# Second attention: value-sum matmuls of a unit in one block, exponentials in two buffers, x parked in DRAM

## What is computed

```python
c_q  = x @ Wq_down                                    # 512 -> 64
c_kv = x @ Wkv_down
q_c = (c_q @ Wq_up).reshape(b, s, 128, 4)
q_r = (x @ Wq_rope).reshape(b, s, 128, 64)
k_c = (c_kv @ Wk_up).reshape(b, s, 128, 4)
v_c = (c_kv @ Wv_up).reshape(b, s, 128, 4)
k_r = x @ Wk_rope                                     # shared by all heads
scores = (einsum('bqhd,bkhd->bhqk', q_c, k_c) + einsum('bqhd,bkd->bhqk', q_r, k_r)) / sqrt(68)
out = einsum('bhqk,bkhd->bqhd', softmax(scores), v_c).reshape(b, s, 512) @ Wo
x = x + ga * out
```

## Time and profile before

| | us |
|---|---|
| median of 3 runs | 2480.24 |
| range of the runs | 2477.19 to 2480.72 |
| span of the profiled execution | 2475.1 |
| TensorE busy (matmuls) | 2315.8 (94%) |
| VectorE busy | 1807.3 (73%) |
| ScalarE busy | 1336.2 (54%) |
| GpSimd busy | 580.5 (23%) |

### The profile page before, as it was taken

How to read it: one execution, slowest core, us unless ns; L and a number is a source line. 1 busy time by engine, 2 the same in 40 slices (tenths; PEclk the granted TensorE clock), 3 DMA queues, 4 the chain that set the end, 5 groups by cost and what they waited for, 6 DMA issues and landing times.

```text
span 2475.1 us, 41157 instructions
## 1 busy us (share of the span) xinstructions
PE 2315.8 (94%) x11084; PEld 1674.6 (68%) x11084; DVE 1807.3 (73%) x3372; ACT 1336.2 (54%) x2583; POOL 580.5 (23%) x428
## 2 busy tenths in 40 slices
PE   6898898998998788999999999999999999999988
PEld 4677777777776555666666666666666666666655
DVE  6788889888887465676676776776776766767856
ACT  2333333333333324776676766766766766766641
POOL 4355545455544041000000000000000000001432
PEclk9899999999999888999999999999999999999998
DMA  5101001001003204111111111111111111112330
GB/s 192 44 26 43 17 25 42 17 25 42 17 0 86 79 1 155 33 38 38 36 37 37 33 36 38 36 37 37 32 37 38 36 37 33 37 37 69 107 82 35
DMA packets 114848, 113.31 MB, mean 46 GB/s; under 512 B 28669, under 2 KB 71197, under 8 KB 114796
## 3 DMA queue, kind: packets, MB, share of 16 engines
q1 hardware_dynamic: 114796, 112.66, 15.4%
HBM read 93.20 MB, written 18.87 MB: 45 GB/s over the span
## 4 chain that ended last, share of the span: by engine, by line
PE 73%; DVE 15%; ACT 4%; issue 3%; DMA 1%; SPq 1%; POOL 1%; DVEq 0%; POOLq 0%; ACTq 0%
PE bank L1773 11%; PE bank L1786 10%; PE bank L1799 10%; PE bank L1787 9%; PE bank L1761 5%; PE bank L1759 5%; PE bank L1760 5%; PE bank L1485 4%; PE bank L1487 4%; PE bank L1486 4%; ACT probs L817 3%; DVE probs L1147 3%; DVE probs L1134 2%; DVE nmax L1138 2%; PE bank L1573 2%
## 5 line engine op out<-in xcount | busy, mean ns | idle before, releaser
L1334 DVE TENSOR_REDUCE mcol<-bank 128x1 fp32r<-128x512 f32 x1024 | 702.3, 690 | 393.3 <-PE bank L1773 386.5
L958 ACT ACTIVATE pT<-bank 128x512 f32<-128x512 f32 x1024 | 598.9, 599 | 368.4 <-PE bank L1787 340.8
L1773 PE MATMUL bank<-km,q 128*128 128x512 f32 x1024 | 434.8, 426 | 5.7 <-DVE mcol L1334 3.4
L1786 PE MATMUL bank<-q,k 128*128 128x512 f32 x1024 | 418.5, 409 | 6.6 <-DVE c_lo L1305 3.2
L1773 PEld LDWEIGHTS bank<-km,q 128*128 128x128 f32 x1024 | 316.8, 310 | 155.5 <-DVE mcol L1334 113.1
L1787 PE MATMUL bank<-q,k 128*128 128x512 f32 x1024 | 405.8, 396 | 0.0
L697 POOL TENSOR_TENSOR wr_lo<-wst,wr_hi 128x512 fp32r<-128x512 f32 x64 | 82.6, 1291 | 1267.1 <-DVE wr_hi L1293 1267.1
L1786 PEld LDWEIGHTS bank<-q,k 128*128 128x128 f32 x1024 | 195.7, 191 | 131.0 <-ACT pT L958 108.2
L1799 PE MATMUL bank<-pT,vp 128*32 128x512 f32 x2048 | 272.7, 605 | 0.7 <-ACT pT L958 0.7
L1787 PEld LDWEIGHTS bank<-q,k 128*128 128x128 f32 x1024 | 192.8, 188 | 37.8
L1761 PE MATMUL bank<-hT_hi,wr_lo 128*128 128x512 f32 x512 | 207.0, 404 | 0.0
(11 more groups left out here) (266 smaller groups left out, 4056.8 us busy)
## 6 DMA issues: line engine op xcount, KB each, us to landing
wst<-in_L_attn_Wq_rope SPq DMA_DIRECT2D x64, 256.0 KB, 3.0
wm<-in_L_wmod SPq DMA_DIRECT2D x12, 1024.0 KB, 8.6
st_q<-in_L_attn_wq SPq DMA_DIRECT2D x8, 1024.0 KB, 7.4
st_wo<-in_L_attn_wo SPq DMA_DIRECT2D x8, 1024.0 KB, 5.2
km<-kc_d SPq DMA_DIRECT2D x256, 32.0 KB
q<-qc_d SPq DMA_DIRECT2D x256, 32.0 KB
k<-kc_d SPq DMA_DIRECT2D x256, 32.0 KB
o_d<-ost SPq DMA_DIRECT2D x512, 16.0 KB
```

What stands on the lines that cost most here:

```text
L958: act.activation(pT[:, s], bank[s % 4][:], ACT.Exp, scale=float((HD1 + ROPE) ** -0.5)).then_inc(exp1, 1)
L1334: dve.tensor_reduce(mcol[:, k % 2, i % 4, i // 4:i // 4 + 1], bank[4 + i % 2][:], AX.X, ALU.max, negate=True)\
L1773: pe.matmul(bank[4 + i % 2][:], q2[:, k % 4, h, i % 4:S:4], km[:, b, h], start=True, stop=True).then_inc(max_mm, 1)
L1786: pe.matmul(bank[s % 4][:], k1[:, k % 2, t], q1[:, k % 4, h], start=True, stop=False)
```

## The change

Two exponential buffers are used in turn: pT, and x's place, PT = (x, pT). So x is stored to DRAM (x_d) after its last addition and loaded back when the last unit that uses it has been summed. On TensorE the two blocks of sums become one of eight matmuls, sum_unit(u - 1), in period u. pv1 counts one for each unit instead of two. The order of TensorE's period is written anew around it. On ScalarE the copy to ost goes from ahead of slot 2 to ahead of slot 3, and on VectorE values goes from ahead of the maxima to behind them.

```diff
+    x_d = scratch("x_d", (P, NT, D))
+        PT = (x, pT)
     SP, ahead of the second attention:
+            sp.wait_ge(f_added, NT)
+            for t in range(NT):
+                sp.dma_start(x_d[:, t], x[:, t]).then_inc(x_moved[0], 16)
     SP, behind the last sums:
             load_last_sums(1)
+            sp.wait_ge(pv1, UNITS - 1)
+            for t in range(NT):
+                sp.dma_start(x[:, t], x_d[:, t]).then_inc(x_moved[1], 16)
     GpSimd, ahead of the additions to x:
+            pool.wait_ge(x_moved[1], 16 * TB + 16 * NT)
     ScalarE:
+            act.wait_ge(x_moved[0], 16 * TB + 16 * NT)
-                    if s == 2:
+                    if s == 3:
                         if exists(u - 1, UNITS):
-                            act.wait_ge(pv1, 2 * u + 1)
+                            act.wait_ge(pv1, u)
                     if exists(u, UNITS):
                         act.wait_ge(scores1, 8 * u + s + 1)
-                        wait(act, pv1, 2 * u + s // 4)
-                        act.activation(pT[:, s], bank[s % 4][:], ...)
+                        wait(act, pv1, u - 1)
+                        act.activation(PT[k % 2][:, s], bank[s % 4][:], ...)
     VectorE:
-                    wait(dve, pv1, 2 * v - 1)
+                    wait(dve, pv1, v - 1)
-                values(u + 1, k + 1, pair(1))
                 maxima(u + 2, k + 2, pair(2), n)
+                values(u + 1, k + 1, pair(1))
     TensorE:
-            def sum_slots(u, k, c):
+            def sum_unit(w, k):
+                if exists(w, UNITS):
+                    pe.wait_ge(exp1, 8 * w + 12)
+                    pe.wait_ge(vp_ready, w + 1)
+                    wait(pe, o_copied, w)
+                    for s in range(8):
                         h, kb = SLOTS[s]
                         j = 2 * h + kb % 2
+                        e = pe.matmul(bank[7][32 * j:32 * j + 32, :], vp[:, k % 2, kb, h], PT[k % 2][:, s], start=(s < 4), stop=(s >= 4))
                     e.then_inc(pv1, 1)
-            pe.sem_inc(pv1, 1)
+                scores(0)
+                scores(1)
+                queries(0)
+                maximum(0)
+                scores(2)
+                maximum(1)
+                sum_unit(u - 1, k - 1)
+                scores(3)
+                maximum(2)
+                scores(4)
+                queries(1)
+                maximum(3)
+                scores(5)
+                maximum(4)
+                queries(2)
+                scores(6)
+                maximum(5)
+                scores(7)
+                maximum(6)
+                queries(3)
+                maximum(7)
```

More of the change, by code:

```diff
@@ L268, in adaln_two_layers @@
         GATE_CHUNKS = (2, 5)
-        x_loaded = [sem(f"x_loaded{b}") for b in range(B)]
+        x_moved = [sem(f"x_moved{b}") for b in range(B)]
         ident_loaded, cond_loaded, rope_loaded = (sem(n) for n in ("ident_loaded", "cond_loaded", "rope_loaded"))
@@ L361, in _ @@
             for t in range(NT):
-                sp.dma_start(x[:, t], x_in[:, t]).then_inc(x_loaded[t // TB], 16)
+                sp.dma_start(x[:, t], x_in[:, t]).then_inc(x_moved[t // TB], 16)
             def load_wmod(l, c):
@@ L956, in period @@
                         act.wait_ge(scores1, 8 * u + s + 1)
-                        wait(act, pv1, 2 * u + s // 4)
-                        act.activation(pT[:, s], bank[s % 4][:], ACT.Exp, scale=float((HD1 + ROPE) ** -0.5)).then_inc(exp1, 1)
+                        wait(act, pv1, u - 1)
+                        act.activation(PT[k % 2][:, s], bank[s % 4][:], ACT.Exp, scale=float((HD1 + ROPE) ** -0.5)).then_inc(exp1, 1)
             for u in range(-3, 6):
@@ L1053, in norm_stats @@
                     if ph == 0:
-                        dve.wait_ge(x_loaded[b], 16 * TB)
+                        dve.wait_ge(x_moved[b], 16 * TB)
                     else:
@@ L1356, in period @@
                     split_rope_weights(pair(4), (k // 2) % 2, quad(4))
+                maxima(u + 2, k + 2, pair(2), n)
                 values(u + 1, k + 1, pair(1))
-                maxima(u + 2, k + 2, pair(2), n)
             for u in range(-3, 6):
@@ L1797, in sum_slots @@
                         h, kb = SLOTS[s]
                         j = 2 * h + kb % 2
-                        e = pe.matmul(bank[7][32 * j:32 * j + 32, :], vp[:, k % 2, kb, h], pT[:, s], start=(c == 0), stop=(c == 1))
+                        e = pe.matmul(bank[7][32 * j:32 * j + 32, :], vp[:, k % 2, kb, h], PT[k % 2][:, s], start=(s < 4), stop=(s >= 4))
                     e.then_inc(pv1, 1)
-            pe.sem_inc(pv1, 1)
             def period(u, k, pair):
[L1806 to L1827, removed]
@@ new lines, in scores, with maximum, queries @@
+                def scores(s):
+                    scores1_slot(u, k, s, pair(0))
+                def maximum(i):
+                    max_scores(u + 2, k + 2, i, pair(2))
+                def queries(kk):
+                    rope_queries(u + 3, k + 3, pair(3), [kk], kk == 0, kk == KT - 1)
+                scores(0)
[5 more added lines that the diff above has]
+                sum_unit(u - 1, k - 1)
```

## The result

The changed kernel takes 2784.01 us (median of 6 runs, 2771.44 to 2793.24), the kernel before 2480.48 (6 runs, 2477.19 to 2482.55): a ratio of 1.1222, with a 95% interval of 1.1202 to 1.1241. The time rose by 303.5 us; the forecast was 344. The profiled execution is one of the two shortest, with a span of 2769.7 us.

What follows compares the result with a forecast made beforehand. TensorE was taken to bound the kernel. Queries with the block's saving +220, last units -1, clock +118, x's reload +5 and reciprocals +2 made +344 on the median 2480: 2824 us, range 2690 to 2880.

Steps and rivals of the forecast that it cites:

- the stall: Second attention: TensorE's first rotary query matmul waits for VectorE's q_low, costing 2.22 us in each of 125 units.
- What bounds the kernel: Second attention: TensorE is the bound, busy 99.86 of 100 us; a unit's 10.87 us have no idle left over.
- step 1: Value sums on TensorE: one block of eight replacing two of four saves 0.46 us per unit (0.12 to 0.46).
- Rival D: Value sums on TensorE: the block of eight keeps two blocks' price, 0.34 us more per unit, 2867 us; chance 0.06.
- step 2: TensorE's first rotary queries, moved ahead, wait for q_low; with the block's saving, 1.76 us more per unit, 220 us.
- step 3: Granted clock in the second attention: idle of 1.95 us per unit brings 75 falls, 118 us (0 to 198).
- Rivals B: Second attention: the stall comes but the granted clock holds, 2706 us; chance 0.16.
- E: Second attention: the granted clock falls in every unit, 2903 us; chance 0.06.
- step 4: x to DRAM and back: store hidden, reload delays the tables and first gated tile by 5 us (3 to 9).
- step 5: Remaining changes cost nothing, except VectorE's reciprocals delaying q_low in six late units: +2 us (0 to 7).
- rival A: Main forecast for the second attention: the stall plus clock falls in 35 to 85% of units, 2824 us (2760 to 2880); chance 0.62.
- Rival C: Second attention: q_low ends before TensorE asks, under 1.8 us; units 0.46 us shorter, 2427 us; chance 0.05.

Runs made afterwards that it cites:

- the first two experiments: Changed kernel with its rotary queries put back later in TensorE's order: 2446.70 us; kernel before with only its first queries moved ahead: 2824.30 us.
- the run with seven fillers: Changed kernel plus seven matmuls per unit, results overwritten unread, between scores 1 and the first queries: 2692.04 us, ratio 1.0866 to the kernel before.
- The last experiment: Changed kernel with TensorE's period reordered: scores 0 to 3, maxima 0 and 1, block of eight, scores 4, maximum 2, then first queries: 2433.72 us.

## Why the prediction was nearly right

The direction, the mechanism and the place were right, the range (2690 to 2880) held the time, and the forecast was 40 us (1.4%) too high. The two terms that were mis-sized are the stall (0.13 us per unit too much) and the number of clock falls (75 in place of 53); the price of the tail and of the late units was too low, and part of the errors cancel. By its steps:

**What bounds the kernel.** Right for TensorE and its steps. "With no idle left over" passed over one thing: every fourth unit, TensorE is later by some 0.3 us where the loop of four periods returns. The mean of 96 units of the kernel before is 10.95, not 10.87. It is paid before and after alike, so it changes no difference.

**The block (step 1).** 0.46 us per unit was forecast. In the timeline above, the way from 1510.93 to 1513.45 is 2.52 us, less two steps of 0.232 is 2.06, as worked out; and cutting the block costs 0.48 per unit. Rival D falls. The lower bound of 0.12 wasn't needed: the sets do follow each other without a gap.

**The first queries (step 2).** The wait, its releaser and the number of units were right, and the first two experiments show that this move makes the loss. Its size was 0.13 too high, which is 16 us in 125 units. The prediction put q_low's end at 3.45, with 0.21 for the copy of the values, "VectorE has no gap there". It has none, but the copy starts at 1507.70, before the transposition ahead of it ends (1507.45 + 0.41 = 1507.86), and so q_low ends at 3.25, only 0.01 later than without the copy. That is 0.20 less. Against it, the way from q_low's end to the waiting matmul is 0.13 and not 0.06. The stall is 3.38 - 1.39 + 0.10 = 2.09 in place of 2.22. The error is that the copy was added at its own length, though it stands between the two ends that the prediction had given; the lower one, 3.24, was the right one. An ordinary unit at full clock is 12.45 us, against 12.63. What the copy's move is for, the prediction didn't ask: undoing it costs 48 us.

**The clock (step 3).** Forecast were 75 falls and 118 us (0 to 198). The profiled execution has 53 low stretches, and the clock costs about 90 us, the difference to the run with seven fillers. The mechanism and the price of one fall were right: by the profiled executions the falls cost 83 us, 1.57 each, against 1.58. The share was too high: 0.6 was taken from four in six idle stretches of 1.80 us and more. Behind waits of 1.84 us it was 27 in 50, close to that, but only every other unit waits so long; behind the others, 1.52 to 1.85 us long, it was 18 in 63. Each stretch lasts 198 / 53 = 3.7 us on average, most of them the 3.4 read before. Rivals B (no fall) and E (a fall in each unit) lie on both sides of what came. The rule of the Trainium skill, page "TensorE: Matmul & The Clock Gate", section "HAM oscillation", that only longer idle matters, didn't hold here: with waits of 1.52 to 1.84 us the clock fell in two units of five. With 1.0 to 1.4 us in each unit it held. Another section of the same page, "A second HAM failure mode: psum-queue depth-cycling", tells of another kernel, in which short idle stretches between groups of matmuls come often and make the clock swing; this trace agrees (53 low stretches), and the prediction had not weighed it.

**x in DRAM (step 4).** +5 was forecast, bounds 3 to 9. Alone it costs 3 to 5 us (3 by the ratio, 4.6 by the medians). In the changed kernel VectorE's wait for the tables is

```profile
2689.89 0.14 DVE L1405 CAST emap<-emap_i 15x1 f32<-15x1 int32 x1 [9.94 <-DMA before<-in_entry_before]
```

6.1 us more than in the earlier trace rows, and the time from the start of the last block of sums to GpSimd's first addition to x is 31.1 in place of 24.1 us. 0.9 of these 7.0 us is the longer block. The store was hidden, as the place of the earlier trace rows said.

**The rest (step 5).** The reciprocals on VectorE were priced at +2, with 7 as the upper bound; they cost about 6. A late unit of the changed kernel:

```profile
2567.07 0.95 DVE L1334 RECIPROCAL dnm<-dnm 128x128 f32<-128x128 f32 x1 [0.77 <-POOL dnm L719]
2567.94 0.63 DVE L1345 TENSOR_REDUCE mcol<-bank 128x1 fp32r<-128x512 f32 x1
2568.49 0.93 DVE L1334 RECIPROCAL dnm<-dnm 128x128 f32<-128x128 f32 x1
...
2571.19 0.79 PE L1770 MATMUL bank<-hT_hi,wr_hi 128*128 128x512 f32 x1 [3.75 <-DVE q L1326]
```

The wait is twice the ordinary one. Count a unit from one scores 0 to the next (lines 1786 and 1797). Units 119 to 124 take 70.5 us in all before, 90.8 with seven fillers and 100.1 in the changed kernel. Ordinary units differ by 1.58, which is 9.5 us for six. Of the 20.3 us between the first two numbers, 4.8 are three low stretches that the fillers leave, and the other 6.0 are the reciprocals. The changed kernel's further 9.3 are the clock again, which falls in nearly every one of these units.

**The sum.** By the profiled executions, whose spans are 294.6 us apart: the chain in 125 units 196 (1.57 each); the reciprocals 6; the clock 69 in the first 118 units (1546.2 us, against 1476.9 with fillers) and 14 in the last ones, 83; the three last units +3, where -1.4 was forecast; the tail behind the last sums 8; and the attention starts 2 us earlier. That makes 294, so nothing of size is left over. The forecast had 220 and 118 for the first and the third of these. The runs of the changed kernel lie up to 22 us apart, and the longer ones have a lower mean clock (0.941 at 2771.44, 0.935 at 2793.24), so the number of falls can make most of the spread. The range of rival A was also worked out loosely: falls in 35 to 85% of 125 units give 2775 to 2874 us, not 2760 to 2880.

**Rival C,** the faster side, decided where q_low ends before 1.8 us; it ended at 3.25. Its number, 2427 us, is what the change would take with the wait covered. The last experiment reaches 2434, 7 us above it. It took three orders of the period to get there.

## What to carry to other kernels

When steps of an in-order engine are mixed anew, write down for each that waits what releases it and how long that chain takes from its own start in the unit before: if it comes back to the same engine, the steps that stand between are its cover, and a step moved ahead of its cover delays every unit, with all engines half idle and none of them the bound. Price such a stall twice, once as time and once as the granted clock behind it; where the stall can't be removed, matmuls to fill it can be worth having. And when a copy is moved along with a larger change, ask whose buffer it waits for before calling the move a cost.

## What the runs showed of the hardware

- Waits of the same 1.84 us were followed by a fall to 1.2 GHz in 27 cases of 50; others, of 1.52 to 1.85 us, in 18 of 63. Two or seven matmuls with unread results in each unit kept the clock at 2.4 GHz in all but the last ten units and saved 86 and 92 us. In those last units, with waits of up to 3.3 us, two matmuls left six low stretches.
- VectorE started a copy of 128x32 0.16 us before the 128x128 transposition ahead of it ended.
- Where a matmul's data came just in time, its weight load came late (0.18 us of idle ahead of it), and the next start was 0.15 us later (0.38 in place of 0.23).
- With eight transfers from ScalarE's queue under way, the load that waits for a store from SP's queue began 5.2 us behind that store's last issue, in place of 2.1 (one trace against one).
